# Two placements in a four-layer attention and expert kernel: the scratch of the splits, and the loads of the expert tables

## The reference

```
x = x + tanh(g_xattn[0]) * xattn0(layernorm(x), ctx)   # 16 heads of 8, masked softmax, Wo, biases
x = x + tanh(g_ffn[0])   * experts0(layernorm(x))      # 6 experts, top 1, softmax over 100 tokens, exp/log
x = x + tanh(g_xattn[1]) * xattn1(layernorm(x), ctx)   # 8 heads of 64, softmax, Wo, bias
x = x + tanh(g_ffn[1])   * experts1(layernorm(x))      # router on the mean, top 2 of 8 experts, gelu, layernorm
```

## Time and profile before

| | us |
|---|---|
| median of 3 runs | 209.82 |
| lowest, highest | 209.39, 210.12 |
| profiled execution, its own time | 210.06 |
| span of the profiled execution, first to last instruction | 208.0 |
| PE busy | 181.6 (87%) |
| DVE busy | 145.6 (70%) |
| ACT busy | 122.0 (59%) |
| POOL busy | 103.8 (50%) |

### The profile page before, as it was taken

The page is one execution under the profiler, slowest core; times in us unless marked ns, Lnnn a source line. Parts: engine busy times, 40 slices in busy tenths (PEclk is TensorE's granted clock), DMA queues, the critical chain, the costliest instruction groups (busy, mean ns, idle before and its releaser), DMA issues.

```text
span 208.0 us, 4451 instructions
## 1 busy us (share of the span) xinstructions
PE 181.6 (87%) x1564; PEld 131.8 (63%) x1564; DVE 145.6 (70%) x361; ACT 122.0 (59%) x315; POOL 103.8 (50%) x152
## 2 busy tenths in 40 slices
PE   0899989598299989798999999898999999999990
PEld 0777554255155645565676767765976868988980
DVE  1374698779449785548958769488978867848574
ACT  3346624554257768579877686378759974064250
POOL 7230000247244547448773489559958866271212
PEclk9999999759959999999999999999999999999998
DMA  5788995907600000000000000000051061527110
GB/s 146 190 235 192 296 178 141 197 14 136 123 0 8 2 3 3 0 3 0 3 0 0 6 0 0 0 3 0 0 190 44 2 165 66 156 75 213 40 50 25
DMA packets 14672, 15.11 MB, mean 73 GB/s; under 512 B 1703, under 2 KB 12044, under 8 KB 14652
## 3 DMA queue, kind: packets, MB, share of 16 engines
q1 hardware_dynamic: 14292, 14.75, 28.1%
q10 hardware_dynamic: 360, 0.10, 0.3%
HBM read 11.11 MB, written 3.67 MB: 71 GB/s over the span
## 4 chain that ended last, share of the span: by engine, by line
PE 59%; DVE 22%; POOL 6%; DMA 5%; issue 3%; ACT 2%; SPq 1%; POOLq 0%; DVEq 0%; ACTq 0%
PE PS L1284 6%; PE PS L1342 5%; PE PS L1332 5%; DVE XH L732 5%; DVE MX L764 5%; PE PS L1300 5%; PE PS L1271 4%; DMA COL<-in_cols 4%; PE PS L1257 4%; PE PS L1148 3%; PE PS L1087 3%; PE PS L1082 3%; PE PS L1312 3%; POOL RS L429 2%; PE PS L1043 2%
## 5 line engine op out<-in xcount | busy, mean ns | idle before, releaser
L471 POOL TENSOR_TENSOR POOLED<-POOLED,RC 128x512 f32<-128x512 f32 x32 | 33.1, 1054 | 10.3 <-DVE RC L876 10.3
L460 POOL TENSOR_SCALAR_AFFINE_SELECT PT<-PT 128x512 f32<-128x512 f32 x16 | 10.2, 635 | 46.5 <-ACT PT L578 46.5
L764 DVE TENSOR_REDUCE MX<-PS 128x4 f32<-128x1024 f32 (+1 forms) x24 | 28.3, 1219 | 6.3 <-PE PS L1112 6.1
L660 ACT ACTIVATE POOLED<-PS,NM 128x256 f32<-128x256 f32 x64 | 29.4, 481 | 5.1 <-DVE NM L867 2.7
L578 ACT ACTIVATE PT<-PS 128x768 f32<-128x768 f32 x32 | 25.4, 810 | 10.0 <-PE PS L1129 6.8
L732 DVE TENSOR_SCALAR XH<-X,MV,RS 128x128 f32<-128x128 f32 x32 | 16.7, 565 | 8.0 <-POOL RS L429 8.0
L867 DVE TENSOR_REDUCE NM<-PS 128x4 f32<-128x1024 f32 x16 | 19.5, 1217 | 3.5 <-PE PS L1271 3.4
L428 POOL TENSOR_SCALAR VE<-MV 128x2 f32<-128x2 f32 x20 | 4.9, 246 | 31.1 <-DVE MV L717 18.1
L691 ACT ACTIVATE POOLED<-PS,BI 128x256 f32<-128x256 f32 x32 | 12.5, 474 | 11.5 <-PE PS L1332 9.7
L1271 PE MATMUL PS<-KT,VA 64*128 64x256 f32 x128 | 17.8, 399 | 0.2
L1284 PE MATMUL PS<-CST,POOLED 128*128 128x128 f32 x128 | 16.9, 275 | 0.0
(11 more groups left out here) (149 smaller groups left out, 405.5 us busy)
## 6 DMA issues: line engine op xcount, KB each, us to landing
POOLED<-in_w SPq DMA_DIRECT2D x8, 512.0 KB, 4.5
POOLED<-qk_scr SPq DMA_DIRECT2D x8, 384.0 KB, 5.8
qk_scr<-POOLED SPq DMA_DIRECT2D x8, 192.0 KB, 2.9
qk_scr<-POOLED SPq DMA_DIRECT2D x8, 128.0 KB, 3.4
W<-in_w SPq DMA_DIRECT2D x3, 256.0 KB, 4.0
BI<-in_bias SPq DMA_DIRECT2D x8, 66.0 KB, 3.6
qk_scr<-POOLED SPq DMA_DIRECT2D x8, 64.0 KB, 3.2
out_x<-X SPq DMA_DIRECT2D x4, 128.0 KB, 1.8
```

The costliest lines, as they stand in the source:

```text
L471: g_.tensor_tensor(pr, pr, RC1[:, n % 2, 2 * h:2 * h + 2].unsqueeze(2).to_broadcast([P, 2, S]), ALU.mult).then_inc(s_p1p, 1)
L660: last = a.activation(PR[n % 3][:, h, it, :], pair("sc", n)[:, h * 512 + it * S:h * 512 + (it + 1) * S], ACT.Exp, bias=NM1[:, n % 2, 2 * h ...
L764: v.tensor_reduce(MX0[:, b, it, :, hw * k:hw * (k + 1)], pair("S", n).rearrange("p (r h j) -> p r h j", r=2, h=hw), AXX, ALU.max, negate=T ...
```

## The change

1. RES moves from PT0 to block 11 of POOLED, the place that W12[0] takes later.
2. The wait of `e0:1:0` on `s_parts` is taken out.
3. In SP's list `te` moves from behind `wo:1` to behind `so:1:2`.

No instruction is added or removed on an engine. From L573 on the lines of the changed kernel are two lower.

```
-so:0:0 so:0:1 so:0:2 w1:0 c:2 si:0 so:1:0 so:1:1 so:1:2 so:2:0 so:2:1
+so:0:0 so:0:1 so:0:2 w1:0 c:2 si:0 so:1:0 so:1:1 so:1:2 te so:2:0 so:2:1
 si:1 so:2:2 vec so:3:0 shift:0 si:2 so:3:1 wo:0 so:3:2 shift:1
-si:3 wo:1 te shift:2 shift:3 w12:0
+si:3 wo:1 shift:2 shift:3 w12:0

-        RES = PT0F[:, 2048:3072].rearrange("p (a n) -> p a n", a=2)
+        RES = BIGF[:, 11264:12288].rearrange("p (a n) -> p a n", a=2)

             def exps0(n, i):

-                if n == 1 and i == 0:
-                    act.wait_ge(s_parts, B)
                 if n >= 3 and i == 0:
                     act.wait_ge(s_av0, n - 2)
```

More of the change, by code:

```diff
@@ L108 @@
 SP_ORDER = table("""
-x:0 w0 c:0 cm w1:1 x:1 w1:2 x:2 one c:1 so:0:0 so:0:1 so:0:2 w1:0 c:2 si:0 so:1:0 so:1:1 so:1:2 so:2:0 so:2:1
-si:1 so:2:2 vec so:3:0 shift:0 si:2 so:3:1 wo:0 so:3:2 shift:1 si:3 wo:1 te shift:2 shift:3 w12:0 w12:1 w12:2
-w12:3 outd:0 outd:1 outd:2 outd:3
+x:0 w0 c:0 cm w1:1 x:1 w1:2 x:2 one c:1 so:0:0 so:0:1 so:0:2 w1:0 c:2 si:0 so:1:0 so:1:1 so:1:2 te so:2:0 so:2:1
+si:1 so:2:2 vec so:3:0 shift:0 si:2 so:3:1 wo:0 so:3:2 shift:1 si:3 wo:1 shift:2 shift:3 w12:0 w12:1 w12:2 w12:3
+outd:0 outd:1 outd:2 outd:3
 """)
```

## The result

The changed kernel took 202.89 us as the median of 4 runs (201.46 to 203.81); the kernel before, now with 4 runs, 209.6 us (208.64 to 210.12). The ratio is 0.968, with a 95% interval of 0.961 to 0.975. The forecast was 204.2, the range 202.3 to 206.2. In two later comparisons on other chips the changed kernel stood at 0.974 (0.969 to 0.978) and 0.973 (0.969 to 0.977) of before. So the gain is 6.7 us in the first comparison, and 5.5 and 5.7 us in the others, where 5.6 was forecast. The profiled execution took 203.13 us with a span of 201.1.

The account below looks back on a forecast made before the run. The chain was taken to run through the late COL load, stalling ACT, PE and DVE, plus low PE clock and the s_parts gate. Terms 0.5 + 3.5 + 1.6 = 5.6 us took 210.06 to 204.5, median 204.2 us; range 202.3 to 206.2.

Parts of the forecast that it names:

- The gate: ACT no longer waits on s_parts for lo:3 on DVE; S:11 on PE starts 1.15 us earlier.
- si:1 late: Five te issues on SP delay the si:1 load by 1.3 us, so S:6 on PE starts 0.7 us late.
- The upper bound: All te issuing and transfer stand ahead of si:1: si:1 3.1 us late, S:6 2.5 us late.
- The wait on COL: COL arrives before oTc:0 on ACT needs it; wo0:0 on PE starts 3.5 us earlier, of a wait of 3.86.
- The clock behind it: From wo0:0 to mx:18, PE's clock does not fall after the shortened wait; 1.6 us more gained.
- The first dip: PE's low clock, 0.50 from 41 to 46 us; the forecast sum counted no gain there.
- both dips go: Rival: PE's low clock from 41 to 46 us vanishes too, saving perhaps 1.8 us more; time 202.4; chance 0.13.
- The clock stays low: Rival: PE's clock stays low behind the shortened wait or falls elsewhere; gain 4.0 us, time 205.8; chance 0.14.
- Slower: Rival: te's five issues take 6.7 us in a full queue, S:6 7.1 us late; time 210.7; slower or no change 0.04.

Follow-up runs that it names:

- one pair above: Kernel before with only te moved early, 30.00 us from mx:0 to wo0:0, against the changed kernel's first trace, 28.84 us.
- the other: Changed kernel with ACT's wait on s_parts kept, 29.39 us from mx:0 to wo0:0, against te behind vec, 27.57 us.
- WTD alone: Changed kernel with only WTD (128 KB, one issue) behind so:1:2, COL behind vec, other three tables behind wo:1: 203.71 us, 0.973 of before.
- COL alone: Changed kernel with only COL behind so:1:2, the other four tables behind wo:1: 201.96 us, 0.964 of before; second round 202.97 us, 0.968.
- The filler: Kernel before plus 8 throwaway 128x256 matmuls on PE while it waits for COL: 207.88 us, 0.989 of before.
- te behind vec: Changed kernel with te moved behind vec in SP's list: 202.35 us, 0.966 of before; second round 202.17 us, 0.964.

## Why the prediction was right, step by step

- **The gate, 1.15 us forecast: right.** 1.16 by one pair above, 1.5 by the other; S:11 hangs on T:2:0 without a gap, as the step had it.
- **si:1 late, S:6 0.7 us late (bounds 0.5 and 2.5): right in kind, too small by 0.5.** S:6 waits 1.04 to 1.28 us in the changed kernel's three traces and starts 1.1 to 1.3 us late from mx:0, and the price is 1.2 to 1.3. I had si:1 1.3 us late; measured from mx:0 it lands 1.85 us later (9.35 instead of 7.5). Its first issue came 1.5 us later from mx:0, where I had counted 1.1. te took 2.1 us as forecast, but began 0.2 us later from mx:0 than so:2:0 did before, and the four issues behind it took 2.02 us, not 1.9. Then the first issue of si:1 took 1.22 us for 0.33, which holds up the second. I had counted issues at one price, though the earlier trace rows shows 0.34 to 1.33. With WTD alone in te's place the landing hardly moved (7.9 us after mx:0, 7.8 with COL alone), so nothing here shows a cost of the tables' bytes. The upper bound, by which the tables' transfer stands ahead of si:1, was not met.
- **The wait on COL, 3.5 us: right.** The idle time fell from 3.86 to 0.34 us, which is 3.52.
- **The clock behind it, 1.6 us: right, somewhat small.** In the trace mx:18 gained 1.55 us more than wo0:0 (6.54 - 4.99). The filler shows 2.1 us to the end of the span: mx:18 comes 1.70 us earlier from mx:0 (34.93 instead of 36.63), and the last 0.39 lie in ln:1:0, 0.91 us instead of 1.30, which I had left as it was.
- **The first dip, left as it was in the forecast: wrong.** The sum had no term for it, only the rival of both dips. It is shorter by half in the first trace of the changed kernel and absent in the two others. Up to wo0:0 the first trace gained 4.04 us from mx:0 (32.88 - 28.84). Less the 3.52 of COL and the 1.16 to 1.5 of the gate, and with the 1.27 that si:1 took added, 0.3 to 0.6 us are left for the dip; in the other two traces it is 1.2 to 1.8. So in the first trace the term that I left out and the 0.5 us by which si:1 was too small cancel, and that is luck: ln:1:0, forecast near 57.8, is at 56.87, which is 57.82 with the 0.95 us of the start put back.
- **The start: no term, rightly.** The 0.95 us of the first pair of traces is the execution's, not the kernel's. The clock moves the medians too: the four executions of the first comparison had a mean granted clock of 0.994, the six of each later one 0.984 and 0.986. That goes with 202.89 in the first and 204.0 and 203.4 in the later ones. The profiled executions of the later two had the highest or nearly the highest clock of their six (0.999 and 0.996), so traces without a dip are not the usual case of this kernel.

Of the rivals, "both dips go" is half true: it holds in two of three traces, and those are of executions with high clocks. "The clock stays low" did not show behind wo0:0: in no trace without the wait on COL is the clock low from 52 to 60 us. Four such traces have it low near 80 us, though. "Slower" fell by its condition: the five issues took 2.1 us, not 6.7.

## What to carry to other kernels

Look at what a small load stands behind, not at its size: 1 KB queued behind two larger steps of SP stopped three engines for 3.5 us. Put it where the issuing engine is idle, not merely early: the same five issues cost 1.2 us ahead of a transfer that someone waits for, and nothing that shows some 6 us later. Price a wait of TensorE twice, by its length and by the clock of the work behind it.

## What was not expected of the hardware

- The clock fell without a long wait of PE. In the trace before it is 1.00 until 39 us and 0.50 from 40, and the gaps of PE ahead of it are 0.26, 0.46 and 0.63 us. In the changed kernel the same gaps stand ahead of the same place (0.25, 0.46, 0.63), and the clock falls a little later in one execution and not at all in two. Four traces show a low clock near 80 us (0.91 from 80 to 100 us with WTD alone), where the first trace of the changed kernel has 1.00. Over its 16 executions the changed kernel's mean clock went from 0.975 to 1.00. So a fall here comes in one execution of a kernel and not in another, worth 1.1 to 1.5 us each, and one trace per kernel doesn't tell whether a change removed it.
- Filling a wait with matmuls whose result is thrown away made the kernel 2.3 us faster.
- The clock row says 1.00 for the first 12 us in every trace, though the same eight matmuls took from 1.89 to 3.32 us there, 0.38 us each or 0.63. With nine matmuls put ahead of them they took 1.89. The likely reading is a low clock that the row doesn't show; no run tells it from another cause.
- An issue of si:1 took from 0.33 to 1.29 us on SP. When the long one happens is not settled: with te behind vec, the same list gave 0.33 and 1.29 in one trace and 0.33 and 0.43 in another; with COL alone in te's place both were short, in both traces.
